# Two transformer layers on one core: GpSimd's power for the first reciprocal deviations, another order around the layers' seam, and small state products

## The chip, the cores and the metric

One core of one Trainium2 chip runs the whole program. The metric is the device time of one execution in microseconds (us). It is given as the median of several executions. TensorE is called PE here, VectorE DVE, ScalarE ACT, GpSimd POOL and SyncE SP, as in the profile.

## The reference

16 sequences of 256 tokens, 128 channels, go through two layers in float32. Each layer adds to its input an attention part and a part of eight experts, both of the normalised input:

```python
xn = _layernorm(x)                               # (x - mean) / sqrt(var + 1e-5)
x = x + attention_softmax_causal_16_heads(xn) + experts_top2_of_8(xn)
xn = _layernorm(x)
# layer 1, first part: retention with a decay, 8 heads of 16 channels
scores = einsum('bnhd,bmhd->bhnm', q, k) * decay[h, n - m]   # causal
ret = einsum('bhnm,bmhd->bnhd', scores, v)       # normalised per head, then gated and projected
out = (silu(xn @ W1) + ret * gn_w + gn_b) @ W2
# layer 1, second part: all 8 experts on all tokens, weighed by gates
probs = softmax(xn @ Wr + br)                    # gate = probs where the sorted running sum < 0.8
y = relu(xn @ W1[e] + b1[e]) @ W2[e] + b2[e]     # 128 -> 512 -> 128, for each e
x = x + out + sum_e gate[e] * y[e]
```

## The kernel before

All work is written out by hand. Each of the five engines has its own program, and counters (semaphores) tie them together: `pe.wait_ge(f_lo, n - 2)` holds PE and all that stands behind it on PE. An engine's order is therefore the order of its code.

**Layer 0** runs in 64 groups of four heads (`G0 = 64`), four groups to a sequence, in numbered slots. Each engine's `slot(g)` does its part of group g or of its neighbours: PE the scores, DVE the row maxima (`row_max_late`, `row_max_early`), ACT the exponential of a group into `probs`, POOL the causal cut of it (`cut_off`), PE the product with the values (`weigh`). Slots 0 to 9 also choose the two best experts of every token on DVE and POOL (`mark_best`, `pick_first`, `choose`, `count`; `COUNT` and `MARK` say in which slots). The experts of layer 0 come between groups 38 and 39 (`middle`). Six more slots (`TAIL0`, 64 to 69) finish the last groups, and the first normalised sequences of layer 1 are already made there.

**Layer 1's normalisation** takes the variance of 24 token tiles at once (`EARLY`, sequences 0 to 11) and of the last 8 later (`LATE`). In the kernel before, `deviation1` takes the root of it on ACT, which loads ACT's table for the square root first. `shift_of` takes the reciprocal on DVE, and `normalise(b, u)` applies it on ACT.

**Layer 1** is a row of 256 units, `UNITS = NB * E * FC`: 8 blocks of 512 tokens, 8 experts, 4 chunks of 128 hidden channels. `hidden(n)` is three products of 512 columns (a float32 product as three products of high and low parts), ACT takes the relu (`hidden_unit`, `f_h`), DVE the rest that f_h leaves (`split_unit`, `f_l`), and `output(n)` is three products more. `hidden(n)` waits for `f_lo >= n - 2`, so it is at most three units ahead of DVE. Sixteen units are a window, in which one sequence's retention is woven in between the units (`between`, by the table `when`): `scores1`, `products_qk`, `products_p`, `weigh1`, `sum_state` and so on. `sum_state` makes the product of keys and values of a sequence's first half, a 128x128 product of which `own_head` keeps the eight 16x16 blocks on the diagonal, and `weigh1` multiplies the queries by it.

**The expert weights of layer 1** come one expert after another over SP's queue, in code order: `load_raw(e, 0)`, then `w1_first` for e (one buffer; it waits for `centred`, the subtraction on POOL that uses it up), then `load_raw(e, 1)`. POOL's `centre(e)` subtracts `w1_first`, ACT's `high_w1(e)` rounds, POOL's `low_w1(e)` takes the rest. The gates of a block are worked out by a chain over POOL, DVE and ACT (`add_bias`, `less_max`, `exponentials`, `gate_sum`, `weigh_probs`, `compare`, `order_probs`, `keep_experts`), go out to memory (`keep_gates`), and come back spread over all partitions, 256 KB for each expert (`load_gate`). The first `LATER` experts of block 0 are multiplied by their gates afterwards on POOL (`gate_later`).

## Time and profile before

| | |
|---|---|
| median of 3 executions | 781.25 us (780.51 to 782.44) |
| the profiled execution's own time | 780.9 us |
| span of its trace | 779.1 us |
| busy PE, DVE, ACT, POOL | 718.4, 557.7, 441.0, 349.7 us |
| granted clock of PE, mean | 0.976 of full speed |

The span runs from the first to the last instruction of the trace; the execution's own time has 1.8 us around it. The matmuls' ends are modelled, so a PE that is shown busy is not always at its peak.

### The profile page before, as it was taken

To read this page: it belongs to the slowest core of one execution; us is meant where nothing else is said; L and a number is where in the kernel's file an instruction comes from. 1 tells how busy PE (TensorE), PEld (TensorE's weight loads), DVE (VectorE), ACT (ScalarE), POOL (GpSimd) and SP (SyncE) were. 2 spreads that over 40 slices of the span, in tenths; PEclk is the share of its full clock that TensorE was granted. 3 is DMA by queue.
4 is the path that set the end of the run, shared out by engine and by line. 5 is a ranking of instruction groups with operands and counts; after the bars stand their busy time and mean duration, and the time that the engine had idled before them with its cause. 6 is when DMAs were issued, how large, how long until landed. Compare 5 with 4: busy or idle time off the path is not lost.

```text
span 779.1 us, 16902 instructions
## 1 busy us (share of the span) xinstructions
PE 718.4 (92%) x5932; PEld 528.3 (68%) x5932; DVE 557.7 (72%) x1151; ACT 441.0 (57%) x821; POOL 349.7 (45%) x497
## 2 busy tenths in 40 slices
PE   5788788998899977779999999999999999999997
PEld 4644445556755536657877877877877878877775
DVE  6877997885688845549767767767767767776674
ACT  5745665775576665366555565565555555554442
POOL 3765644783758875176224224225224224223222
PEclk9998999999999988979999999999999999999999
DMA  6974655431144442531200210310410410400310
GB/s 189 266 222 133 177 143 201 149 106 41 59 123 124 122 131 64 127 122 41 70 30 12 83 39 5 82 42 1 82 42 1 92 33 2 95 28 12 85 42 14
DMA packets 64243, 66.85 MB, mean 86 GB/s; under 512 B 6689, under 2 KB 42273, under 8 KB 64161
## 3 DMA queue, kind: packets, MB, share of 16 engines
q1 hardware_dynamic: 62560, 63.40, 28.8%
q0 software_dynamic: 1024, 2.12, 1.0%
q8 instruction: 49, 0.80, 0.4%
q10 hardware_dynamic: 576, 0.27, 0.1%
q14 instruction: 34, 0.27, 0.1%
HBM read 47.62 MB, written 17.99 MB: 84 GB/s over the span
## 4 chain that ended last, share of the span: by engine, by line
PE 70%; DVE 8%; POOL 7%; DMA 5%; issue 3%; ACT 3%; SPq 2%; POOLq 0%; ACTq 0%; DVEq 0%
PE ps L1890 24%; PE ps L2096 22%; DVE m L1350 3%; PE ps L2007 2%; PE ps L1809 2%; PE ps L1713 2%; DMA qk_parts<-qk_p 2%; DMA w_first<-in_w_first 2%; POOL probs L696 2%; POOL x L679 2%; PE ps L1958 2%; PE ps L1923 1%; PE ps L1723 1%; PE ps L1719 1%; PE ps L2023 1%
## 5 line engine op out<-in xcount | busy, mean ns | idle before, releaser
L1571 DVE SCALAR_TENSOR_TENSOR f_l<-ps,f_h 128x512 fp32r<-128x512 f32 x256 | 176.0, 688 | 133.7 <-ACT f_h L1064 133.1
L1064 ACT ACTIVATE f_h<-ps 128x512 fp32r<-128x512 f32 x256 | 152.6, 598 | 182.1 <-PE ps L1890 178.1
L1890 PE MATMUL ps<-x_hl,w_h 128*128 128x512 f32 x512 | 194.6, 401 | 11.7 <-DVE f_l L1571 10.1
L829 POOL TENSOR_TENSOR acc<-acc,yt 128x512 f32<-128x512 f32 x56 | 72.7, 1298 | 196.9 <-DVE yt L1588 196.8
L1890 PEld LDWEIGHTS ps<-x_hl,w_h 128*128 128x128 f32 x512 | 98.0, 191 | 36.9 <-DVE f_l L1571 11.3
L969 ACT ACTIVATE probs<-ps 128x1536 f32<-128x1536 f32 x64 | 92.9, 1451 | 39.3 <-PE ps L1732 38.7
L2096 PE MATMUL ps<-f_h,w_h 128*128 128x512 f32 x256 | 108.1, 422 | 0.0
L696 POOL TENSOR_SCALAR_AFFINE_SELECT probs<-probs 128x512 f32<-128x512 f32 x128 | 78.7, 640 | 64.9 <-ACT probs L969 64.7
L1890 PE MATMUL ps<-x_hl,w_l 128*128 128x512 f32 x256 | 102.4, 400 | 0.0
L2096 PE MATMUL ps<-f_h,w_l 128*128 128x512 f32 x256 | 102.1, 399 | 0.0
L2096 PE MATMUL ps<-f_l,w_h 128*128 128x512 f32 x256 | 101.3, 396 | 0.0
L1350 DVE TENSOR_REDUCE m<-ps 128x4 f32<-128x1024 f32 x64 | 78.0, 1219 | 9.7 <-PE ps L1723 9.6
L2096 PEld LDWEIGHTS ps<-f_h,w_h 128*128 128x128 f32 x256 | 48.5, 190 | 12.8 <-issue 3.2
L1890 PEld LDWEIGHTS ps<-x_hl,w_l 128*128 128x128 f32 x256 | 49.2, 192 | 11.0
L2096 PEld LDWEIGHTS ps<-f_l,w_h 128*128 128x128 f32 x256 | 48.5, 189 | 11.8
L2096 PEld LDWEIGHTS ps<-f_h,w_l 128*128 128x128 f32 x256 | 48.7, 190 | 7.5
L1588 DVE SCALAR_TENSOR_TENSOR yt<-ps,b,gate_b 128x512 f32<-128x512 f32 x54 | 40.5, 750 | 6.3 <-PE ps L2096 3.1
L1343 DVE TENSOR_REDUCE m<-ps 128x4 f32<-128x512 f32 x64 | 43.5, 680 | 0.4 <-PE ps L1719 0.4
L1508 DVE TENSOR_TENSOR sc<-ps,upto 128x512 f32<-128x512 f32 x64 | 43.6, 681 | 0.0
L1809 PE MATMUL ps<-probs,v_ring 128*16 128x256 f32 x512 | 41.4, 395 | 0.7 <-ACT wvn L951 0.5
L1732 PE MATMUL ps<-q_st,k_st 49*128 49x128 bf16 x256 | 36.2, 222 | 2.9 <-DMA q_st<-m_neg 2.9
L1713 PE MATMUL ps<-mask_qk,ident_h 128*128 128x256 bf16 x128 | 25.5, 281 | 14.6 <-DVE m L1350 12.2
(234 smaller groups left out, 1349.8 us busy)
## 6 DMA issues: line engine op xcount, KB each, us to landing
gate_b<-gate_rows SPq DMA_DIRECT2D x64, 256.0 KB, 3.6
qk_parts<-qk_p SPq DMA_DIRECT2D x16, 512.0 KB, 3.8
k_st<-qk_parts SPq DMA_DIRECT2D x64, 96.0 KB
q_st<-qk_parts SPq DMA_DIRECT2D x64, 96.0 KB
y_tok<-zero SPq DMA_DIRECT2D x8, 512.0 KB, 3.0
w_raw<-in_w_e SPq DMA_DIRECT2D x16, 256.0 KB, 3.2
x_rows<-xn_rows SPq DMA_DIRECT2D x8, 260.0 KB, 3.4
w_up<-in_w_up SPq DMA_DIRECT2D x8, 256.0 KB, 2.7
```

The source lines that it names most:

```text
L696: nc.gpsimd.affine_select(tiles, tiles, pattern=[[0, GH], [1, P]], compare_op=ALU.is_ge, fill=0.0, base=0, channel_multiplier=-1)\
L829: nc.gpsimd.tensor_tensor(acc[:, j % 2, :], acc[:, j % 2, :], yt[:, i % 3, :], ALU.add).then_inc(summed, 1)
L969: nc.scalar.activation(probs[:, at(g, HELD), :, :], ps[:, 3:6, :], ACT.Exp, scale=float(D) ** -0.5)\
L1064: nc.scalar.activation(r32(f_h[:, n % 4, :]), ps[:, n % 3, :], ACT.Relu).then_inc(f_hi, 1)
L1343: nc.vector.tensor_reduce(m8[:, at(g, 2), :, 0], ps[:, first, :].rearrange("p (h k) -> p h k", h=GH), AX.X, ALU.max).then_inc(early_max, 1)
L1350: nc.vector.tensor_reduce(m8[:, at(g, 2), :, 1], ps[:, first + 1:first + 3, :].rearrange("p c (h k) -> p (c h) k", h=2), AX.X, ALU.max).th ...
L1508: nc.vector.tensor_tensor(sc[:, h, :, :], ps[:, 4 + h, :].rearrange("p (k t) -> p k t", t=P), upto[:, :].unsqueeze(1).broadcast_to([P, 4, ...
L1571: nc.vector.scalar_tensor_tensor(out=r32(f_l[:, n % 4, :]), in0=ps[:, n % 3, :], scalar=0.0, in1=f_h[:, n % 4, :], op0=ALU.max, op1=ALU.su ...
L1713: nc.tensor.matmul(scores_at(g)(c).rearrange("p (h k) -> p h k", h=2)[:, :, P:S], ident_h[:, :], mask_qk[:, :].unsqueeze(1).broadcast_to([ ...
L1809: nc.tensor.matmul(ps_o[32 * h:32 * h + 2 * HD0, :], v_ring[:, u, 0, k * GH + h, :], probs[:, at(g, HELD), 1 + h // 2, h % 2 * S:(h % 2 + ...
L1890: last = nc.tensor.matmul(dst, r32(lhs[i]), r32(rhs[j]), start=(k == 0), stop=(k == 2))
L2096: last = nc.tensor.matmul(ps[:, 3, :], r32(w[i]), r32(fs[:, n % 4, :]), start=(c == 0 and k == 0), stop=(c == FC - 1 and k == 2))
```

## The change

Layer 0's choice of experts is spread over one slot more (`COUNT` 5, `MARK` 10, `mark_best` and `pick_first` in slots 0 to 3). The reciprocal deviations of `EARLY` are one instruction on POOL, `var` to the power of -0.5; the variance of `LATE` moves to DVE's unit 29 and its root to ACT's unit 34, behind a root that ACT takes there anyway. The first sequences of layer 1 are normalised, turned and multiplied among the last slots. The two products with the state become four products of 32 channels each. On SP, `keep_gates(0)` and the first gate loads move behind the loads of experts 5 and 6, and on POOL the later gating moves from unit 13 to units 17 to 20. Some banks of PSUM are given out anew. Cut to its core:

```diff
-COUNT = 4
-MARK = 9
+COUNT = 5
+MARK = 10
-LATER = 3
+LATER = 4
...
-        def ps_t1(b): return ps[:, b if b < 2 else 0 if b == 2 else 4, 0:S]
+        def ps_t1(b): return ps[:, b if b < 2 else 3 if b == 2 else 4, 0:S]
-        def bank_p1(b): return 4 if b in (0, 2) else 6
-        def ps_state(b): return ps[:, 4 if b == 0 else 7, 0:P]
+        def bank_p1(b): return 4 if b in (0, 2) else 0 if b == 1 else 6
+        def ps_state(b): return ps[:, 6 if b == 0 else 7, 0:2 * HD1]
...
-            usual = {"values_by_scores": 9, "turn_z": 8, "put_z": 11, "put_o": 12, "turn_o": 12, "project": 13, "heads": 15,
+            usual = {"values_by_scores": 8, "turn_z": 8, "put_z": 11, "put_o": 12, "turn_o": 12, "project": 12, "heads": 15,
...
-                if e == 3:
+                if e == 5:
                     keep_gates(0)
+                if e == 6:
                     for k in range(4):
                         load_gate(0, k)
-                if e >= 5:
-                    load_gate(0, e - 1)
-            load_gate(0, E - 1)
+            for k in range(4, E):
+                load_gate(0, k)
...
+                if num(g) == G0 - 4:
+                    nc.gpsimd.memset(minus_half[:, :], -0.5).then_inc(padded, 1)
+                if num(g) == G0 - 1:
+                    pool.wait_ge(padded, 1)
+                    pool.wait_ge(var_ready, 1)
+                    nc.gpsimd.tensor_tensor(rstd[:, EARLY], var[:, EARLY], minus_half[:, 0:1].broadcast_to([P, EARLY.stop]), ALU.pow).then_inc(rstd_ready, 1)
+                    add_experts(B - 1)
+                    centre(0)
...
             values(0)
+            low_w1(1)
+            put_ones(0)
             add_bias(0)
             less_max(0)
-            put_ones(0)
-            low_w1(1)
+            values(1)
             weigh_probs(0)
-            values(1)
             order_probs(0)
...
-                        if n == max(FC * e - 10, 0):
+                        if n == (0, 2, 6, 12, 16, 20)[e - 2]:
                             centre(e)
...
-                if n == 13:
-                    for g in range(LATER):
+                for g in range(LATER):
+                    if n == (17, 17, 19, 20)[g]:
                         gate_later(g)
                         add_expert(g)
...
+                if num(g) == G0 - 1:
+                    act.wait_ge(rstd_ready, B + 2)
+                    normalise(0, 0)
                 if within(g, G0):
                     act.wait_ge(st_done, num(g) + 1)
...
                 if num(g) == G0:
-                    deviation1(1, EARLY)
+                    high_x(0)
+                    normalise(1, 1)
...
-            deviation1(2, LATE)
             put_gate(0)
+            halve(0)
             high_w1(1)
-            halve(0)
+            put_gate(1)
             high_x(2)
-            put_gate(1)
...
                     root_of(b)
+                    if b == 1:
+                        deviation1(2, LATE)
...
+                if n == G0 - 1:
+                    shift_of(1, EARLY)
+                if n == LAST - 1:
+                    dve.wait_ge(late_in, (LATE_IN + 5) * 16)
+                    put_qk(0)
+                    put_values(0)
+                    put_qk(1)
...
-                if n in (1, 2):
-                    pick_first(n - 1)
-                if n in (0, 1):
-                    mark_best(n)
+                if n in (1, 3):
+                    pick_first(n // 2)
+                if n in (0, 2):
+                    mark_best(n // 2)
...
-                if n == G0 - 2:
+                if n == G0 - 3:
                     variance_of(EARLY)
...
+                if n == 29:
+                    for b in range(B - 2, B):
+                        stats_of(b)
+                    variance_of(LATE)
+                if n == 38:
+                    shift_of(2, LATE)
...
-                nc.tensor.matmul(ps_state(b), k_tok[:, b % 2, :], v1[:, b % 4, 0, 0:D], start=True, stop=True).then_inc(state_mm, 1)
+                for h in range(GH):
+                    pair = slice(32 * h, 32 * h + 32)
+                    last = nc.tensor.matmul(ps_state(b)[pair, :], k_tok[:, b % 2, pair], v1[:, b % 4, 0, pair], start=True, stop=True)
+                last.then_inc(state_mm, 1)
...
-                nc.tensor.matmul(ps_o1[:, P:S], states[:, b % 3, :], qk1[:, b % 3, 0, P:S], start=False, stop=False, skip_group_check=True)
+                for h in range(GH):
+                    pair = slice(32 * h, 32 * h + 32)
+                    nc.tensor.matmul(ps_o1[pair, P:S], states[pair, b % 3, :], qk1[pair, b % 3, 0, P:S], start=False, stop=False, skip_group_check=True)
...
-            products_qk(0)
-            products_p(0)
             products_qk(1)
+            products_p(1)
             transposes(2)
+            hidden(0)
+            hidden(1)
             pe.wait_ge(x_attn, B)
-            products_p(1)
             sum_state(0)
-            pe.wait_ge(state_put, 1)
+            pe.wait_ge(v1_put, 1)
             products_p(2)
             sum_state(1)
-            hidden(0)
-            hidden(1)
```

`shift_of(1, ...)` no longer takes the reciprocal itself, and `memset` of `v1_ring` stays where it was. `normalise(1, 1)` and `high_x` are each a slot or two earlier in the tail.

**PE, the first hidden units.** In the kernel before, PE's rows from the last products of sequence 2 on (`w1_p` with `x_hl` is `products_p`, `w1_h` and `w1_l` with `x_hl` are hidden units, `k_tok` is `sum_state`):

```order
L1984 MATMUL ps<-v1,k_tok 128x128 [waits v1_put,k_put]
L1890 MATMUL ps<-x_hl,w1_h 128x512 [waits xl_put,ones_put,w1_lo]
L1890 MATMUL ps<-x_hl,w1_l 128x512
L1890 MATMUL ps<-x_hl,w1_h 128x512 x2
L1890 MATMUL ps<-x_hl,w1_l 128x512
L1890 MATMUL ps<-x_hl,w1_h 128x512
L1890 MATMUL ps<-x_hl,w1_h 128x512 [waits qk1_put]
L1890 MATMUL ps<-x_hl,w1_l 128x512
L1890 MATMUL ps<-x_hl,w1_h 128x512
L1890 MATMUL ps<-x_hl,w1_h 128x512 [waits f_lo]
L1890 MATMUL ps<-x_hl,w1_l 128x512
L1890 MATMUL ps<-x_hl,w1_h 128x512
```

In the changed kernel, the rows in the same place behind `hidden(1)`:

```order
L1995 MATMUL ps<-v1,k_tok 32x32 x3
L1899 MATMUL ps<-w1_p_hi,x_hl 128x392 [waits xl_put,v1_put]
L1899 MATMUL ps<-w1_p_hi,x_hl 128x392
L1899 MATMUL ps<-w1_p_lo,x_hl 128x392
L1899 MATMUL ps<-w1_p_hi,x_hl 128x264 x2
L1899 MATMUL ps<-w1_p_lo,x_hl 128x264
L1995 MATMUL ps<-v1,k_tok 32x32 [waits v1_put,k_put]
L1995 MATMUL ps<-v1,k_tok 32x32 x3
L1899 MATMUL ps<-x_hl,w1_h 128x512 [waits qk1_put]
L1899 MATMUL ps<-x_hl,w1_l 128x512
L1899 MATMUL ps<-x_hl,w1_h 128x512
L1899 MATMUL ps<-x_hl,w1_h 128x512 [waits f_lo]
```

The products of sequence 2 stood ahead of `hidden(0)` and `hidden(1)` and now stand between `hidden(1)` and `hidden(2)`; the last row is `hidden(3)`, the first that waits for `f_lo`.

**POOL, the last groups of layer 0.** Before (`probs` rows are the cuts of a group, `y_top` and `xn_rows` the addition of the experts to a sequence, `w1_first` a `centre`, `w1_l` a `low_w1`):

```order
L696 AFFINE_SELECT probs<-probs 128x4x128 [waits exp_done]
L696 AFFINE_SELECT probs<-probs 128x512
L696 AFFINE_SELECT probs<-probs 128x4x128 [waits exp_done]
L696 AFFINE_SELECT probs<-probs 128x512
L679 TENSOR_TENSOR x<-x,y_top 128x256 [waits x1_half,gathered1]
L679 TENSOR_TENSOR x<-x,xn_rows 128x256 [waits x1_half]
L831 MEMSET v1_ring 128x1024
L748 TENSOR_TENSOR w_raw<-w_raw,w1_first 128x512 [waits first_in,raw_in0,padded]
L753 TENSOR_TENSOR w1_l<-w_raw,w1_h 128x512 [waits w1_hi]
L748 TENSOR_TENSOR w_raw<-w_raw,w1_first 128x512 [waits first_in,raw_in2]
```

And now:

```order
L697 AFFINE_SELECT probs<-probs 128x4x128 [waits exp_done]
L697 AFFINE_SELECT probs<-probs 128x512
L716 TENSOR_TENSOR rstd<-var,minus_half 128x24 [waits var_ready,padded]
L680 TENSOR_TENSOR x<-x,y_top 128x256 [waits x1_half,gathered1]
L680 TENSOR_TENSOR x<-x,xn_rows 128x256 [waits x1_half]
L754 TENSOR_TENSOR w_raw<-w_raw,w1_first 128x512 [waits first_in,raw_in0]
L697 AFFINE_SELECT probs<-probs 128x4x128 [waits exp_done]
L697 AFFINE_SELECT probs<-probs 128x512
L838 MEMSET v1_ring 128x1024
L759 TENSOR_TENSOR w1_l<-w_raw,w1_h 128x512 [waits w1_hi,padded]
```

The power, the addition and the first `centre` stand ahead of the last group's two cuts.

**SP, the weights and gates of block 0.** Before, from expert 3's loads on (`w1_first` and the two `w_raw` rows around it are one expert):

```order
L511 DMA w1_first<-in_w1_first 128x512 [waits centred]
L504 DMA w_raw<-in_w2_e 128x512 [waits w2_lo]
L569 DMA gate_rows<-gT 4x8x128 [waits gt_put]
L564 DMA gate_b<-gate_rows 128x512 [waits gates_out]
L564 DMA gate_b<-gate_rows 128x512 x3
L504 DMA w_raw<-in_w1_e 128x512 [waits w1_lo]
L511 DMA w1_first<-in_w1_first 128x512 [waits centred]
L504 DMA w_raw<-in_w2_e 128x512 [waits w2_lo]
L504 DMA w_raw<-in_w1_e 128x512 [waits w1_lo]
L511 DMA w1_first<-in_w1_first 128x512 [waits centred]
L504 DMA w_raw<-in_w2_e 128x512 [waits w2_lo]
L564 DMA gate_b<-gate_rows 128x512 [waits raw_gated,yv]
```

And now, from expert 5's loads on:

```order
L505 DMA w_raw<-in_w1_e 128x512 [waits w1_lo]
L512 DMA w1_first<-in_w1_first 128x512 [waits centred]
L505 DMA w_raw<-in_w2_e 128x512 [waits w2_lo]
L570 DMA gate_rows<-gT 4x8x128 [waits gt_put]
L505 DMA w_raw<-in_w1_e 128x512 [waits w1_lo]
L512 DMA w1_first<-in_w1_first 128x512 [waits centred]
L505 DMA w_raw<-in_w2_e 128x512 [waits w2_lo]
L565 DMA gate_b<-gate_rows 128x512 [waits gates_out]
L565 DMA gate_b<-gate_rows 128x512 x3
L505 DMA w_raw<-in_w1_e 128x512 [waits w1_lo]
L512 DMA w1_first<-in_w1_first 128x512 [waits centred]
L505 DMA w_raw<-in_w2_e 128x512 [waits w2_lo]
```

The gates' way out and the four loads that wait for it stood between experts 3 and 4; they now stand behind expert 5 and behind expert 6.

## Rows read from the trace of the kernel before

**Rows 1.** Windows: busy us of each engine, PEclk is the granted clock.

```profile
core 0 of [0], span 779.1 us
...
330.00:335.00 5.00, 1.11 (x3) 0.92 (x4) 0.69 (x1) 3.37 (x6) 3.07 (x3) 0.50 0.43 141
379.59:408.36 28.77, 28.77 (x194) 23.14 (x194) 19.77 (x38) 16.75 (x31) 6.51 (x11) 1.00 0.19 50
```

**Rows 2.** Timeline of PE, 302 to 350: start, us, work [idle before].

```profile
302.67 0.77 PE L1890 MATMUL ps<-x_hl,w_h 128*128 128x512 f32 x1 [1.62 <-issue]
...
311.70 0.50 PE L1890 MATMUL ps<-x_hl,w_h 128*128 128x512 f32 x1
...
333.88 0.79 PE L1890 MATMUL ps<-x_hl,w_h 128*128 128x512 f32 x1 [7.04 <-DVE f_l L1571]
...
348.58 0.50 PE L1890 MATMUL ps<-x_hl,w_h 128*128 128x512 f32 x1 [3.08 <-DVE f_l L1571]
...
349.47 1.09 PE L2007 MATMUL ps<-qk 16*128 16x128 f32 x16
```

**Rows 3.** Timeline of SP, issues of 318 to 322; then the landing times of w_first.

```profile
318.73 1.96 SPq L564 DMA_DIRECT2D gate_b<-gate_rows  x4
...
321.21 1.10 SPq L511 DMA_DIRECT2D w_first<-in_w_first  x1
...
DMA to landing us min/median/max: 2.7/2.9/9.0
```

**Rows 4.** Timeline of POOL, 284 to 331.

```profile
284.26 1.23 POOL L696 TENSOR_SCALAR_AFFINE_SELECT probs<-probs 128x512 f32<-128x512 f32 x2 [2.98 <-ACT probs L969]
...
301.60 0.98 POOL L761 MEMSET x_hl<- 1x512 f32 x2
302.55 1.27 POOL L753 TENSOR_TENSOR w_l<-w_raw,w_h 128x512 fp32r<-128x512 f32 x1
...
330.30 1.26 POOL L748 TENSOR_TENSOR w_raw<-w_raw,w_first 128x512 f32<-128x512 f32 x1 [14.30 <-DMA w_first<-in_w_first]
```

**Rows 5.** Timeline of ACT, 285 to 347.

```profile
285.86 1.28 ACT L1015 ACT_TABLE_LOAD   x1
...
300.87 0.38 ACT L1049 ACTIVATE sg<-ps 128x256 f32<-128x256 f32 x1 [0.64 <-PE ps L1890]
301.27 1.28 ACT L1098 ACT_TABLE_LOAD   x1
...
346.54 0.23 ACT L1098 ACTIVATE g_x<-g_l 128x32 f32<-128x32 f32 x1 [4.44 <-POOL g_l L791]
```

**Rows 6.** Timeline of DVE, 304 to 312.

```profile
304.05 0.48 DVE L1551 TENSOR_TENSOR g_gt<-g_p 128x256 f32<-128x256 f32 x1 [0.82 <-POOL g_p L796]
...
310.95 0.69 DVE L1571 SCALAR_TENSOR_TENSOR f_l<-ps,f_h 128x512 fp32r<-128x512 f32 x1 [3.00 <-ACT f_h L1064]
```

**Rows 7.** Timelines of DVE and PE, 58 to 61.

```profile
58.26 0.42 DVE L1236 TENSOR_REDUCE r_s<-r_b 128x32 f32<-128x256 f32 x1
...
60.33 0.61 PE L1713 MATMUL ps<-mask_qk,ident_h 128*128 128x256 bf16 x2 [2.56 <-DVE m L1350]
```

**Rows 8.** Chain of waits in one steady window, 395 to 402: start, us, work.

```profile
395.50 0.57 PE ps L2018 x16
396.07 0.42 PE ps L2020 x2
...
397.06 0.91 PE ps L2096 x3
397.97 0.70 PE ps L1890 x3
...
401.69 0.22 PE ps L1984 x2
```

**Rows 9.** Groups of POOL by line and shape, whole run.

```profile
L748 POOL TENSOR_TENSOR w_raw<-w_raw,w_first 128x512 f32<-128x512 f32 x8 | 10.7, 1332 | 16.2 <-DMA w_first<-in_w_first 16.0
...
L785 POOL TENSOR_TENSOR g_l<-v,rb 128x32 f32<-128x32 f32 x8 | 2.0, 254 | 18.7 <-DVE v L1494 18.7
```

82 lines of the change are left out of this document (36 added, 46 removed).

## The prediction

> **What bounds the kernel now.** I read the slices of the page first, then windows, then PE's timeline where they dip. From about 350 us to the end PE has no idle time: a window of sixteen units takes 28.8 us and PE is busy in all of it, at the full clock [rows 1]. Nothing but PE's own work can move that part. Between 282 and 352 us, where layer 0 ends and the weights of layer 1 come in, PE waits again and again, and this is where the change works. Three places count [rows 2]. The first hidden unit starts at 302.67 us, after 1.6 us of idle, at half clock: its first product shows 0.77 us where the same product at 311.70 shows 0.50. At 333.88 PE has been idle for 7.0 us. At 348.58 it has been idle for 3.1 us. The window that starts with `scores1(1)` begins only at 349.47.
>
> The 7.0 us: PE and DVE stand because ACT stands in `high_w1(4)`, which waits for POOL's `centre(4)`, and POOL has been idle for 14.3 us until `w1_first` landed [rows 4]. SP issued that load at 321.21, right behind the four gate loads of 318.73 (1 MB) [rows 3]. It took 9.0 us to land where the median is 2.9 [rows 3]. After it PE works at the lower of its two clocks: 0.50 granted from 330 to 335 [rows 1]. The 3.1 us: ACT waited 4.4 us for POOL's `less_max(1)` before the exponential of the gates, with the relus queued behind it [rows 5]. POOL was late because `centre(4)` was late and because unit 13's gating stands ahead of `less_max(1)` in its code.
>
> **The seam up to the first hidden unit.** Removed from ACT: the load of the square root's table, 1.28 us at 285.86 [rows 5], and its root; from DVE a reciprocal. In their place POOL takes the power of 128x24 numbers. No row shows this operation. From below: an addition of 128x32 takes 0.25 us [rows 9]. From above I take POOL's longest arithmetic row, 1.3 us for 128x512 [rows 9]; a power is more work on each number than a subtraction, so I take the upper value, 1.3 us. It begins when POOL has done the cuts of group 62, at 281.3 us (2.98 us before the row at 284.26) [rows 4]; the variance, moved one slot earlier, is ready before that. Its result is at 282.6, the shift 0.3 us later, and ACT's two normalisations (0.9 us) end at 283.8. Only then does ACT take group 63's exponential, about 1.1 us later than before, and POOL adds 1.5 + 1.3 us (addition, `centre(0)`) ahead of its cuts, which start near 285.5 instead of 284.26. All behind it slips by about 1.2 us, but products, turns and normalisations of sequences 0 and 1 now run in gaps of the tail. I followed each engine's new order with durations of the old rows. `put_gate(0)` ends at 296.8, `low_w1(1)` at 299.2, and `put_ones(0)` (0.98 us [rows 4]), for which `hidden(0)` waits, at 300.2 instead of 302.6. **Term 1: -2.5 us.** PE is idle for some 1.9 us just before, as it was before, so I take the lower clock for the first units again.
>
> **From hidden(0) to hidden(5).** This stretch gets longer. In the kernel before, a chain runs through it: `put_gate(2)` at 300.87 and ACT's table load at 301.27 [rows 5], exponential, sum on DVE, `weigh_probs`, `compare` at 304.05 [rows 6], `order_probs`, `centre(2)`, `high_w1(2)`, relu, the rest of unit 2 at 310.95 to 311.64 [rows 6], then `hidden(5)` at 311.70 [rows 2]. From table load to `hidden(5)` that is 10.4 us, and the load began 1.4 us ahead of `hidden(0)`. Now `products_p(2)`, which `put_gate(2)` needs, stands behind `hidden(0)` and `hidden(1)`. At the low clock these take 2.6 us (two times 0.70 us for three products [rows 8], nearly doubled), `sum_state(0)` 0.4, the 1968 columns of `products_p(2)` 1.7, and `put_gate(2)` 0.4: the table load starts 5.1 us behind `hidden(0)`. The chain is 0.7 us shorter, since `low_w1(1)` (1.27 us at 302.55) no longer stands ahead of `weigh_probs` [rows 4, 6]. So `hidden(5)` follows `hidden(0)` by 5.1 + 9.7 = 14.8 us instead of 9.0. **Term 2: +5.8 us** (3.8 at the full clock). A new wait of PE, of about 3 us, should show before `hidden(3)`, which waits for `f_lo`; `compare(0)` stands ahead of `split_unit(0)` on DVE.
>
> **From hidden(5) to scores1(1).** Before: 311.70 to 349.47, 37.8 us [rows 2]. A steady window gives 28.8 us from one `scores1` to the next [rows 1], 3.3 of them before the unit that answers to `hidden(5)`; the first window also lacks a turn, a projection and a sum, 1.0 us. That makes 24.5 us if nothing waits. Does anything? `w1_first` now meets only the expert loads: `centre(2)`, a load of 2.9 us, `centre(3)`, a load, `centre(4)` ends some 6.5 us behind `hidden(5)`, and ACT comes to `high_w1(4)` 7 us behind it. Each further expert has 7 us of PE's time for a cycle of 4.2. `less_max(1)` stands ahead of the gating now. **Term 3: -13.3 us.** It includes both idle times and the half-speed stretches behind them.
>
> **Window 1.** Before, it began at the low clock and took 1.3 us more than a steady one. The gating is here now: seven instructions of 1.3 us on POOL in units 17 to 20, beside `centre(7)`, the heads and `order_probs(1)`. I count `low_w1(7)` done about 1.2 us before PE needs it for `hidden(28)`. The late statistics give DVE some 1.8 us in unit 29; DVE is busy 19.8 us of a window's 28.8 [rows 1]. **Term 4: -1.3 us.**
>
> **The steady windows.** `weigh1` shows 0.57 us for sixteen instructions, 0.42 for the full-array product with the state and another long row behind [rows 8]. Eight more small instructions at the same 0.036 us would be 0.28: -0.14. `sum_state` costs 0.22 us [rows 8]; as eight small ones 0.28, and 0.2 for changing to small tiles and back, as the 0.91 us against 0.70 show behind `weigh1` [rows 8]: +0.26. The projection now stands with other small products and saves one change, -0.1. The sum is 0.0 a window, give or take 0.12, so ±2 us over 16 windows. **Term 5: 0.**
>
> **Slots 0 to 4.** DVE's `mark_best(1)`, two instructions of 0.42 us, moves from ahead of a row maximum that PE was idle 2.6 us for to behind it [rows 7]. **Term 6: -0.8 us.** Should the clock then not fall, 2 us more come back.
>
> Sum: -2.5 + 5.8 - 13.3 - 1.3 + 0 - 0.8 = -12.1, and 780.9 of the profiled execution becomes 768.8. The median stands 0.35 us above that execution: 769 us, own range 764.5 to 773 (clock at full in term 2, -2; a fall avoided in term 6, -2; windows ±2; the power down to 0.25 us, -1, or up to 3 us, +1.7).
>
> **Rivals.**
> - *The small state products don't overlap.* The four products with the state use rows and columns of one block each and write one bank. Nothing in the trace runs like this: `scores1` uses a bank for each block of rows. If they go one by one, eight at 0.11 us (`sum_state`'s 0.22 for two [rows 8]) are 0.88 instead of 0.42, +0.46 in each of 16 windows: 776.4. Chance 0.12. The Trainium skill speaks for it: TensorEngine Tiling (Array Packing), Gotcha 1: PSUM Pressure, says that different row tiles cannot access the same bank at once. No row here shows it.
> - *The power costs some 6 to 12 us.* Every microsecond over 1.3 delays ACT's last exponential by as much: 774 to 780. Chance 0.1. The Trainium skill (GPSIMD Engine Reference, 2.1 Instruction dispatch) has about 6 us for the first call of a freshly loaded kernel; POOL's first kinds here show no such gap.
> - *The power is slower still, and the change loses.* Place: ACT's wait for `rstd_ready` ahead of group 63's exponential. From 1.3 + 12.1 = 13.4 us on it decides; at 20 us the time is 787.5. For it: the work is some 3,000 powers, and POOL is the only engine of which no root or power is seen. Against it: all its two-operand rows follow their size alone. Chance 0.05.
> - *POOL's backlog moves instead of going.* If the gate loads land 3 us late or the order of units 17 to 22 is tighter than I count, `low_w1(7)` holds PE at `hidden(28)` for 3 to 5 us: 772 to 774. Chance 0.1.
> - *The gate loads were not the cause.* Then `centre(4)` waits as long behind `w1_first` and only terms 1, 2 and 4 act: 780 to 783. Against it: 9.0 us beside a median of 2.9. Chance 0.03.
>
> Forecast 0.6. A difference under 0.3% can't be told from none here. Faster by more: 0.92; within 0.3%: 0.03; slower: 0.05. The range goes from 764.5 to 776.5 us, so that the first rival is in it.
>
> **What would show it.** In the changed profile: the power near 1.3 us at about 281; `hidden(0)` near 300; a wait of 3 us before `hidden(3)`; no wait for `w1_first` over 3 us; `scores1(1)` near 339.5; windows of 28.8 us. The forecast is wrong if the power is long, if a window is 29.2 us or more, or if PE is idle between 315 and 375.

## The result, and the profile of the changed kernel

| | before | changed |
|---|---|---|
| median of 4 executions each, one chip | 781.17 us (780.51 to 782.44) | 775.4 us (774.58 to 777.66) |
| profiled execution, its span | 780.9, 779.1 us | 777.66, 775.9 us |
| busy PE, DVE, ACT, POOL | 718.4, 557.7, 441.0, 349.7 us | 719.5, 558.4, 438.4, 355.2 us |

The medians differ by 5.8 us, where 12.2 were forecast (the ratio is 0.9929, with a 95% interval of 0.9904 to 0.9953). The time is inside the range of 764.5 to 776.5 us, and the sign is right; the size is a little under half.

Five marks on PE split the difference of the two traces, which is only 3.2 us (779.1 to 775.9): the profiled execution of the changed kernel was the slowest of its four. Against the forecast of -12.1 that leaves 8.9 us to explain. The first column of numbers is the kernel before [rows 1, 2], the second the changed one.

| stretch on PE | before | changed | measured | forecast |
|---|---|---|---|---|
| start to scores of group 63 | 281.87 | 277.44 | -4.4 | -0.8 (term 6) |
| from there to `hidden(0)` | 20.8 | 24.9 | +4.1 | -2.5 (term 1) |
| `hidden(0)` to `hidden(5)` | 9.0 | 13.8 | +4.8 | +5.8 (term 2) |
| `hidden(5)` to `scores1(1)` | 37.8 | 24.6 | -13.2 | -13.3 (term 3) |
| window 1 | 30.05 | 34.60 | +4.55 | -1.3 (term 4) |
| `scores1(2)` to the end | 399.6 | 400.6 | +1.0 | 0 (term 5) |

The first mark flatters the change: PE waited 2.94 us for a load ahead of group 63's scores in the kernel before and 1.57 us in the changed one. At the scores of group 62 (277.17 and 274.10 us) the changed kernel is 3.1 us ahead, and from there to `hidden(0)` it takes 28.2 us instead of 25.5, +2.7. Group 63's scores in the kernel before:

```profile
281.87 0.26 PE L1732 MATMUL ps<-q_st,k_st 49*128 49x128 bf16 x1 [2.94 <-DMA q_st<-m_neg]
```

PE's timeline in the changed kernel; start, us, work, and in brackets the idle time before it and what ended it:

```profile
277.44 0.26 PE L1737 MATMUL ps<-q_st,k_st 49*128 49x128 bf16 x1 [1.57 <-DMA q_st<-m_neg]
...
285.77 0.66 PE L1939 MATMUL ps<-ident,wv_tok 128*128 128x128 f32 x2 [6.10 <-ACT o_ring L945]
...
302.30 0.47 PE L1899 MATMUL ps<-x_hl,w_h 128*128 128x512 f32 x1 [1.67 <-POOL x_hl L767]
...
309.38 0.79 PE L1899 MATMUL ps<-x_hl,w_h 128*128 128x512 f32 x1 [3.07 <-DVE f_l L1573]
...
316.10 0.39 PE L1899 MATMUL ps<-x_hl,w_h 128*128 128x512 f32 x1
...
340.67 0.73 PE L2019 MATMUL ps<-qk 16*128 16x128 f32 x16
...
347.38 0.50 PE L2112 MATMUL ps<-f_l,w_h 128*128 128x512 f32 x1 [1.38 <-DVE f_l L1573]
...
350.03 0.79 PE L1899 MATMUL ps<-x_hl,w_h 128*128 128x512 f32 x1 [1.45 <-DVE f_l L1573]
```

The idle times of 7.04 and 3.08 us [rows 2] are gone. In their place stand 6.10 us ahead of 285.77, 3.07 us ahead of `hidden(3)` (309.38, as forecast), and two of 1.4 us in window 1, where none was forecast.

POOL shows the cause of the first, and a part of the last two:

```profile
278.18 4.20 POOL L716 TENSOR_TENSOR rstd<-var,minus_half 128x24 f32<-128x24 f32 x1
...
339.15 1.30 POOL L823 TENSOR_TENSOR acc<-acc,gate_b 128x512 f32<-128x512 f32 x1 [2.66 <-DMA gate_b<-gate_rows]
340.93 1.27 POOL L823 TENSOR_TENSOR yt<-yt,gate_b 128x512 f32<-128x512 f32 x1 [0.48 <-DMA gate_b<-gate_rows]
...
343.53 0.24 POOL L802 TENSOR_TENSOR g_p<-g_x,g_s 128x32 f32<-128x32 f32 x1
...
347.82 1.27 POOL L754 TENSOR_TENSOR w_raw<-w_raw,w_first 128x512 f32<-128x512 f32 x1
```

The power takes 4.20 us, not 1.3. At 339.15 POOL has waited 2.66 us for the gates of the first expert; `weigh_probs(1)` (343.53) and `centre(7)` (347.82) stand behind. On ACT and on DVE:

```profile
283.15 0.88 ACT L1028 ACTIVATE xn_ring<-x,shift,rstd 128x128 f32<-128x128 f32 x2 [6.66 <-DVE shift L1428]
283.94 1.43 ACT L978 ACTIVATE probs<-ps 128x1536 f32<-128x1536 f32 x1
285.26 0.37 ACT L945 ACTIVATE o_ring<-ps 128x256 f32<-128x256 f32 x1
...
349.13 0.63 ACT L1039 ACTIVATE w_h<-w_raw 128x512 fp32r<-128x512 f32 x1 [3.66 <-POOL w_raw L754]
```

```profile
343.81 1.50 DVE L1553 TENSOR_TENSOR g_gt<-g_p 128x256 f32<-128x256 f32 x1 [1.89 <-POOL g_p L802]
345.23 1.50 DVE L1554 TENSOR_TENSOR g_ge<-g_p 128x256 f32<-128x256 f32 x1
346.65 0.68 DVE L1573 SCALAR_TENSOR_TENSOR f_l<-ps,f_h 128x512 fp32r<-128x512 f32 x1
```

ACT stands 6.66 us for the shift, with the exponential of group 63 and the copy of `o_ring` behind it, for which PE waits until 285.77. In window 1, DVE waits for `weigh_probs(1)`, then makes two comparisons of 1.50 us, and only then the rest `f_l` that PE waits for at 347.38; ACT waits 3.66 us for `centre(7)` with the relus behind it, and PE waits a second time. SP tells why the gates were late (the last two lines are SP's next load of `w1_first`, expert 7's, and the time that it took to land):

```profile
334.85 0.33 SPq L505 DMA_DIRECT2D w_raw<-in_w_e  x1
335.22 1.86 SPq L565 DMA_DIRECT2D gate_b<-gate_rows  x4
...
337.61 1.22 SPq L512 DMA_DIRECT2D w_first<-in_w_first  x1
...
DMA to landing us min/median/max: 9.9/9.9/9.9
```

The four gate loads stand behind expert 6's second raw load, which waits for DVE's `low_w2(4)`. Behind the four stands the `w1_first` of expert 7. It was 9.9 us on its way and landed at about 347.5, where the median of the eight is 3.1: what held `centre(4)` in the kernel before [rows 3] now happens to `centre(7)`, which started at 347.82. POOL's rows show no wait for it, because POOL was busy with the late gating until that moment. So `centre(7)` had two causes to be late that end within 0.3 us of each other, the gating ahead of it on POOL and its own load.

Windows (columns as in [rows 1]) show the clock:

```profile
345.00:350.00 5.00, 2.21 (x9) 1.15 (x7) 4.96 (x8) 1.34 (x3) 4.92 (x5) 0.91 0.71 196
350.00:355.00 5.00, 4.97 (x16) 4.19 (x17) 5.00 (x9) 1.88 (x5) 4.76 (x6) 0.50 0.20 52
...
375.27:404.14 28.87, 28.87 (x203) 23.06 (x203) 20.05 (x39) 16.85 (x32) 6.47 (x11) 1.00 0.18 49
```

After the two waits the granted clock is 0.50, the lower level, for five microseconds: window 1 loses 5.7 us against a steady one, 2.8 of them idle; the rest goes with the lower clock. The steady window is 0.10 us longer than before.

### The profile page after: what moved, and what is told of

Same layout as the page of the kernel before. It is cut to its first block, busy times and chain, and to the rows that moved or that the text cites. A ratio compares the mean times of both kernels' runs of the same rounds, so it can differ in the third digit from the quotient of the medians.

```text
span 775.9 us, 17290 instructions
## 1 busy us (share of the span) xinstructions
PE 719.5 (93%) x6124; PEld 528.2 (68%) x6124; DVE 558.4 (72%) x1150; ACT 438.4 (57%) x819; POOL 355.2 (46%) x500
## 4 chain that ended last, share of the span: by engine, by line
PE 74%; DVE 9%; POOL 7%; issue 3%; ACT 3%; DMA 3%; SPq 1%; POOLq 0%; DVEq 0%; ACTq 0%
PE ps L1899 26%; PE ps L2112 23%; DVE m L1354 3%; PE ps L2019 2%; POOL x L680 2%; POOL probs L697 2%; PE ps L1718 2%; PE ps L1814 2%; PE ps L1967 2%; DMA qk_parts<-qk_p 1%; PE ps L1932 1%; PE ps L1728 1%; PE ps L2030 1%; PE ps L2037 1%; PE ps L1724 1%
## 5 line engine op out<-in xcount | busy, mean ns | idle before, releaser
L1814 PE MATMUL ps<-probs,v_ring 128*16 128x256 f32 x512 | 41.4, 395 | 1.6 <-issue 1.1
L1718 PE MATMUL ps<-mask_qk,ident_h 128*128 128x256 bf16 x128 | 25.3, 280 | 13.2 <-DVE m L1354 11.2
```

What stands on the lines that cost most here:

```text
L1718: nc.tensor.matmul(scores_at(g)(c).rearrange("p (h k) -> p h k", h=2)[:, :, P:S], ident_h[:, :], mask_qk[:, :].unsqueeze(1).broadcast_to([ ...
L1814: nc.tensor.matmul(ps_o[32 * h:32 * h + 2 * HD0, :], v_ring[:, u, 0, k * GH + h, :], probs[:, at(g, HELD), 1 + h // 2, h % 2 * S:(h % 2 + ...
```

## The experiments

Kernels of one group below ran on the same chip, each with the kernel before beside it. The chips differ by up to 1.8% in absolute times (the kernel before had medians of 794.2, 780.7 and 794.9 us), so ratios to the kernel before and stretches inside a trace are compared.

**Group 1, price: what a power costs.**

```diff
+            TRIED = ((24, ALU.pow), (6, ALU.pow), (1, ALU.pow), (12, ALU.pow), (96, ALU.pow), (24, ALU.mult))
+                for k, (count, op) in enumerate(TRIED):
+                    if n == 100 + 10 * k:
...
+                            nc.gpsimd.tensor_tensor(tried[:, k, 0:count], var[:, 0:count], minus_half[:, 0:1].broadcast_to([P, count]), op)
```

> The changed kernel with six more instructions on POOL in the steady windows of layer 1, where POOL is idle most of the time, each into a buffer that nobody reads: the power of 128x24, 128x6, 128x1, 128x12 and 128x96 numbers and a product of 128x24. The profile of the changed kernel has one power, 128x24 in 4.20 us. If a power costs by its elements, the five show about 4.2, 1.1, 0.2 to 0.3, 2.1 and 16.8 us. If it costs a fixed time whatever the shape, all five show about 4.2. If the 4.20 us were the price of a first call (code or a table that has to come in), the first one here, which is the second of the program, is far below 4.2, near 0.25 us. The product should show about 0.25 in each case.

Groups of POOL by shape (count, busy us, mean ns):

```profile
L898 POOL TENSOR_TENSOR tried<-var,minus_half 128x96 f32<-128x96 f32 x1 | 15.6, 15636 | 0.0
L896 POOL TENSOR_TENSOR tried<-var,minus_half 128x24 f32<-128x24 f32 x2 | 4.4, 2198 | 0.0
L717 POOL TENSOR_TENSOR rstd<-var,minus_half 128x24 f32<-128x24 f32 x1 | 4.2, 4204 | 0.0
L896 POOL TENSOR_TENSOR tried<-var,minus_half 128x12 f32<-128x12 f32 x1 | 2.3, 2270 | 0.0
L896 POOL TENSOR_TENSOR tried<-var,minus_half 128x6 f32<-128x6 f32 x1 | 1.3, 1337 | 0.0
L896 POOL TENSOR_TENSOR tried<-var,minus_half 128x1 f32<-128x1 f32 x1 | 0.6, 550 | 0.0
```

The two of 128x24 at L896 are a power (4.17 us, the longest) and the product (0.22 us, the shortest). So the cost is 0.16 us for each column and 0.4 us besides, and the second call is as long as the first. A power costs by its elements; it is not the price of a first call. The whole kernel took 801.5 us in its one execution: 16 us of power in window 8 hold up everything (that window took 37.9 us, where a steady one takes 28.9), so such an instruction is not free even where POOL is idle three quarters of the time.

**Group 1, power_first: only six columns ahead of the last group.**

```diff
+        FIRST, SECOND = slice(0, 6), slice(6, EARLY.stop)
-                    nc.gpsimd.tensor_tensor(rstd[:, EARLY], var[:, EARLY], minus_half[:, 0:1].broadcast_to([P, EARLY.stop]), ALU.pow).then_inc(rstd_ready, 1)
+                    power_of(FIRST)
...
+            pool.wait_ge(rstd_ready, B + 2)
+            power_of(SECOND)
             pool.wait_ge(padded, 2)
             low_w1(0)
```

> The changed kernel, where the power ahead of the last group's cuts takes only the six columns that sequences 0 to 2 need, and the other eighteen are done behind the clearing of v1_ring, where POOL was idle for 6.35 us. Cost by elements: the first power takes 1.1 us instead of 4.20, the shift comes at 279.3 instead of 282.4, PE's idle time of 6.10 us shrinks to about 3, hidden(0) starts near 299.2 instead of 302.3, and the end comes 3 us earlier than in the changed kernel (772.4 us if that one is 775.4). Fixed cost: the first power takes 4.2 us again, nothing moves, the same time within 0.5 us. A third reading, that hidden(0) waits for something else at the seam (the weights' rounding, values), would show the power short and hidden(0) still at 301.5 or later: a gain under 1 us.

Measured: 787.34 us, ratio 0.9929 (0.9901 to 0.9956). The powers took 1.37 and 3.22 us, PE's idle time fell to 4.40 us:

```profile
290.18 0.21 PE L1745 MATMUL ps<-q_st,k_st 49*128 49x128 bf16 x1 [1.29 <-DMA q_st<-m_neg]
295.97 0.66 PE L1947 MATMUL ps<-ident,wv_tok 128*128 128x128 f32 x2 [4.40 <-ACT o_ring L952]
...
312.38 0.47 PE L1907 MATMUL ps<-x_hl,w_h 128*128 128x512 f32 x1 [1.68 <-POOL x_hl L772]
```

From the scores of group 63 to `hidden(0)` it is 22.2 us, 2.7 less than the 24.9 of the changed kernel's trace: the forecast of "cost by elements". One pair of traces is weak for that, since the seven traces with the full power spread from 22.8 to 25.0; the table under term 1 below takes the clock apart from it. In the whole time no gain is shown: the ratio is that of the changed kernel (0.9929; 0.994 in `after_again`), where 3 us less would have been 0.989.

**Group 1, gates_ahead: the gate loads before expert 6's second raw load.**

```diff
                 sp.dma_start(w1_first[:, :], a["w1_first"][:, ds(e, 1), :].rearrange("p o f -> p (o f)")).then_inc(first_in, 16)
+                if e == 6:
+                    for k in range(4):
+                        load_gate(0, k)
                 load_raw(e, 1)
...
-                if e == 6:
-                    for k in range(4):
-                        load_gate(0, k)
```

> The changed kernel, where SP issues the four gate loads between expert 6's w1_first and its second raw load, for which SP stands still until 334.85 us. My theory: window 1 lost 5.7 us because POOL waited until 339.15 and 340.93 for gate_b and was then late with weigh_probs(1) (DVE stood 1.89 us) and with centre(7) (ACT stood 3.66 us). With the loads issued at about 330.5 and landed by 335, the first later gating starts near 336.6, centre(7) about 2.8 us earlier, ACT's wait falls under 1 us, PE's two idle times of 1.38 and 1.45 us go or nearly go and the clock does not fall: window 1 takes 29 to 31 us instead of 34.6, and the end comes 4 to 5 us earlier. Rival, the order of POOL's units is too tight whenever the gates come: window 1 stays over 33 us and the gain is under 1.5 us. Rival, the loads now delay w1_first of expert 6 (9.0 us to land in the kernel before): window 0 gets longer than 30.5 us and the sum gains nothing.

Measured: 785.56 us, ratio 0.9895 (0.9872 to 0.9918). POOL and ACT in window 1 (it starts at 352.84 here, 12.2 us later on the clock than in the changed kernel's trace):

```profile
347.37 1.29 POOL L754 TENSOR_TENSOR w_raw<-w_raw,w_first 128x512 f32<-128x512 f32 x1
348.61 1.30 POOL L823 TENSOR_TENSOR acc<-acc,gate_b 128x512 f32<-128x512 f32 x1
349.99 1.30 POOL L823 TENSOR_TENSOR yt<-yt,gate_b 128x512 f32<-128x512 f32 x1
...
357.38 1.30 POOL L754 TENSOR_TENSOR w_raw<-w_raw,w_first 128x512 f32<-128x512 f32 x1
```

```profile
358.72 0.63 ACT L1039 ACTIVATE w_h<-w_raw 128x512 fp32r<-128x512 f32 x1 [1.08 <-POOL w_raw L754]
```

No wait for `gate_b` is left; `centre(7)` follows `centre(6)` by 10.0 us instead of 12.6, ACT's wait falls from 3.66 to 1.08 us, PE idles once in window 1, 0.53 us, and the window takes 29.60 us instead of 34.60. Window 0 stays at 29.66: `w1_first` is not delayed. The order of the units was not too tight. The edit also brings the `w1_first` of expert 7 away from the gate loads: no `w1_first` takes more than 4.8 us to land here. So the run shows that the place of the gate loads costs these us, and does not tell POOL's late gating from the late `w1_first`. The other traces agree: six with the late loads (the changed kernel's two, `price`, `power_first`, `old_choice`, `full_state`) have a window 1 of 33.0 to 34.8 us, six with the early ones (`gates_ahead`, `both`, `exp_first`, `best2`, `best3`, `root_act`) 29.6 or 29.7. In the whole time the ratio is 0.0034 to 0.0045 under the changed kernel's, 2.7 to 3.6 us, less than the 4 to 5 expected.

**Group 1, old_seam: the seam's order as before, in the changed kernel.**

```diff
-                if e == 5:
+                if e == 3:
                     keep_gates(0)
-                if e == 6:
                     for k in range(4):
                         load_gate(0, k)
...
-                        if n == (0, 2, 6, 12, 16, 20)[e - 2]:
+                        if n == max(FC * e - 10, 0):
...
-                    if n == (17, 17, 19, 20)[g]:
+                if n == 13:
+                    for g in range(LATER):
```

> The changed kernel with the order of the seam's weights and gates as before: keep_gates(0) and the first gate loads behind expert 3, the others after experts 5 to 7, centre(e) in the old units, three experts gated later in unit 13. My theory, that this part alone brought the gain of terms 3 and 4: window 0 takes 39 to 42 us again instead of 29.7, with PE idle about 7 us for w1_first, window 1 about 30 us instead of 34.6; the end comes 4 to 7 us later than in the changed kernel, near 780. If instead the loads are not the cause (the tail's order or the choice of slots brought the gain), window 0 stays near 30 us and the time within 1 us of the changed kernel's.

Measured: 800.43 us, ratio 1.0089 (1.0061 to 1.0117), slower than the kernel before. Window 0 took 44.11 us, window 1 30.57: together 74.7, against 64.6 in the kernel `power_first` on the same chip. This order alone is worth 10.1 us net of the late gates. PE idles 7.59 us in window 0 again; POOL waited 14.71 us for a `w1_first` that was issued at 336.18, right behind the four gate loads of 333.69, and landed only at about 345.6. With the old order the rest of the change is a loss of 6 to 7 us, in part because that order costs more here than in the kernel before (window 0 of 44.1 us against 41.4).

**Group 2, both: the two mends together** (the edits of `power_first` and `gates_ahead`).

> The changed kernel with two edits already tried alone: the short first power (hidden(0) 2.7 us closer to the last group's scores) and the gate loads ahead of expert 6's second raw load (window 1 29.6 us instead of 34.6). If the two losses are independent, they add: hidden(0) about 22.2 us behind scores(63) instead of 24.9, window 1 29.6 us, and the end 7.7 us earlier than the changed kernel, a ratio of 0.983 to 0.984 to the kernel before. Rival, that the earlier first unit only makes the expert weights late (they come over one queue): window 0 then grows by 1 to 3 us and the ratio is 0.986 to 0.989.

Measured: 768.53 us, ratio 0.9858 (0.9835 to 0.9882), worse than the 0.983 to 0.984 expected, though on the same chip it is 7.9 us under `full_state` (below), which has neither mend. Group 63's scores to `hidden(0)` 19.9 us, window 0 29.74, window 1 29.56. Both gains stand side by side, and the weights did not become late. The first stretch is 2.3 us shorter than the 22.2 us of `power_first`: 0.9 us of it because the power starts 0.1 us behind group 63's scores and not 1.0, and 1.4 us with the clock: PE's granted clock was back at 0.89 in the second five microseconds behind the idle time, in the other trace 0.50:

```profile
280.00:285.00 5.00, 2.54 (x21) 1.32 (x21) 0.43 (x2) 2.56 (x6) 4.68 (x6) 0.50 0.34 108
285.00:290.00 5.00, 3.68 (x37) 2.71 (x34) 1.61 (x7) 2.96 (x8) 2.73 (x2) 0.89 0.01 2
```

```profile
298.00:303.00 5.00, 3.88 (x35) 2.15 (x28) 0.76 (x3) 1.42 (x4) 2.94 (x1) 0.50 0.03 11
```

**Group 2, exp_first: group 63's exponential ahead of the normalisation** (on top of `both`; POOL's cuts of group 63 move ahead of `add_experts` and `centre(0)` too).

```diff
-                if num(g) == G0 - 1:
-                    act.wait_ge(rstd_ready, B + 2)
-                    normalise(0, 0)
                 if within(g, G0):
                     act.wait_ge(st_done, num(g) + 1)
...
+                if num(g) == G0 - 1:
+                    act.wait_ge(rstd_ready, B + 2)
+                    normalise(0, 0)
```

> The kernel of the last expectation with one more edit: in slot 63 ACT takes the exponential of group 63 ahead of normalise(0, 0), and POOL its cuts ahead of the addition and centre(0), directly behind the short power. In the changed kernel ACT stood 6.66 us there for the shift, with the exponential and the next copies of o_ring behind it. My theory: the copy behind the exponential is what PE waited 6.1 us for (4.4 with the short power); it now comes 3 us earlier, PE idles about 1.5 us there and hidden(0) comes 1.5 to 3 us earlier in relation to scores(63), about 20 us behind it. Rival, the path to hidden(0) goes over the normalised tokens, not over the exponential: PE's idle time moves to the turns of sequence 0 and 1, and hidden(0) comes less than 0.7 us earlier.

Measured: 769.18 us, ratio 0.9855 (0.9833 to 0.9877). PE's idle time for `o_ring` fell to 1.89 us, but `hidden(0)` comes 19.8 us behind group 63's scores, as in `both` (19.9), and the time is the same. My theory fell, the rival holds: the exponential was what PE was seen to wait for, and the chain that sets `hidden(0)` does not go over it. A gain of 0.7 us may hide behind the clock: from the end of the power to `hidden(0)` it is 19.1 us here, against 19.8 in `power_first`, both at the lower clock.

**Group 2, best2: the order around the first units** (on top of `exp_first`).

```diff
+            put_ones(0)
             low_w1(1)
-            put_ones(0)
...
+                if n == 0:
+                    put_gate(2)
+                    exponentials(0)
...
                 split_unit(n)
+                if n == 0:
+                    gate_sum(0)
+                    put_state(1)
+                    compare(0)
```

> The kernel of the last expectation with the order around the first units changed: on POOL put_ones(0), for which hidden(0) waited 1.67 us, ahead of low_w1(1); on ACT put_gate(2) and the exponential of the gates behind the first relu; on DVE gate_sum, put_state(1) and compare behind the first split_unit. My theory of term 2: PE's 3.07 us before hidden(3) are a wait for split_unit(0), which stood behind compare(0) and the gates' chain; it goes (under 0.7 us is left), hidden(0) comes 1.2 us earlier, and scores1(0) comes 3 to 4 us earlier; a ratio of 0.974 to 0.978 if the rest follows. Rival, the weights of experts 2 to 4 hold PE then: the waits of 1.00 and 0.81 us in window 0 grow to 2 to 4 us, window 0 takes 31 to 33 us and less than 1.5 us of the gain is left at scores1(1).

Measured: 769.62 us, ratio 0.9849 (0.983 to 0.9869). PE, then ACT:

```profile
297.26 0.47 PE L1910 MATMUL ps<-x_hl,w_h 128*128 128x512 f32 x1 [0.47 <-POOL x_hl L773]
...
301.93 0.51 PE L1910 MATMUL ps<-x_hl,w_h 128*128 128x512 f32 x1 [0.65 <-DVE f_l L1582]
...
310.41 0.80 PE L1910 MATMUL ps<-x_hl,w_h 128*128 128x512 f32 x1 [4.12 <-DVE f_l L1582]
```

```profile
308.52 0.63 ACT L1047 ACTIVATE w_h<-w_raw 128x512 fp32r<-128x512 f32 x1 [5.36 <-POOL w_raw L760]
```

The ratio is that of `both`, where 0.974 to 0.978 was expected: nothing is gained. The 3.07 us ahead of `hidden(3)` fell to 0.65, as my theory had it, and window 0 grew to 34.58 us, more than the rival had it. The place is another than the rival's: not a load, but ACT's `high_w1(2)`, which stood 5.36 us for `centre(2)`, and that stood on POOL behind the four instructions of `order_probs(0)`. Term 2's wait had covered this one.

**Group 2, full_state: the products with the state at full width, in the changed kernel.**

```diff
-                for h in range(GH):
-                    pair = slice(32 * h, 32 * h + 32)
-                    last = nc.tensor.matmul(ps_state(b)[pair, :], k_tok[:, b % 2, pair], v1[:, b % 4, 0, pair], start=True, stop=True)
-                last.then_inc(state_mm, 1)
+                nc.tensor.matmul(ps_state(b), k_tok[:, b % 2, :], v1[:, b % 4, 0, 0:D], start=True, stop=True).then_inc(state_mm, 1)
```

(and `weigh1`'s product in the same way)

> The changed kernel with the two products with the state as before: one 128x128 product for sum_state and one for weigh1 in place of four of 32 channels each, with the mask and the state at their old sizes; the order of PE's work stays as changed. Windows of the changed kernel take 28.87 and 28.55 us, of the kernel before 28.77 and 28.45. If the small products are the 0.10 us, windows fall to 28.77 and 28.45 here and the time by 1.1 to 1.6 us. If they save and another part of the new order costs, windows rise to 28.95 to 29.2 and the time by 1 to 4 us. If they cost nothing either way, the windows stay at 28.87 and 28.55, and the 0.10 belongs to the moved steps (turn_sum shows 0.59 us where it showed 0.35 to 0.44).

Measured: 776.4 us, ratio 0.994 (0.992 to 0.9959); windows 28.79 and 28.45 us, so the small products are the 0.10 us. From `scores1(2)` to the end it is 399.8 us instead of 400.6; the ratio is too coarse to show this. The chain of waits in a steady window (start, us, work), the changed kernel first:

```profile
397.38 0.20 PE ps L1995 x8
397.57 0.59 PE ps L2075 x4
398.16 0.45 PE ps L2065 x4
...
419.31 0.35 PE ps L2034 x8
```

```profile
398.80 0.22 PE ps L1993 x2
399.02 0.44 PE ps L2070 x4
399.46 0.45 PE ps L2060 x4
...
420.58 0.42 PE ps L2029 x2
```

Eight small instructions of `sum_state` show 0.20 us, the full ones 0.22; in `weigh1` 0.35 and 0.42. What is lost stands behind: `turn_sum`, the first full product after the small ones, shows 0.59 instead of 0.44.

**Group 3, after_again: the changed kernel as the measure.**

> The changed kernel itself once more, as the measure for the other three on the same chip. Expected: a ratio of 0.993 to the kernel before; scores(63) to hidden(0) about 24.9 us, window 0 29.7 us, window 1 34.6 us.

Measured: 789.68 us, ratio 0.994 (0.9918 to 0.9962). Scores of group 63 to `hidden(0)` 23.8 us, windows 29.87 and 32.98: the first and the last are 1.1 and 1.6 us shorter than in the first trace of the same kernel. PE's granted clock was back earlier (0.86 against 0.50 in the five microseconds from 13 us ahead of `hidden(0)`; 0.80 against 0.50 behind the waits of window 1). A difference of 1.5 us between two traces in these stretches need therefore be no effect of an edit.

**Group 3, old_choice: the choice of experts in the old slots.**

```diff
-COUNT = 5
-MARK = 10
+COUNT = 4
+MARK = 9
...
-                if n in (0, 2):
-                    mark_best(n // 2)
+                if n in (0, 1):
+                    mark_best(n)
```

> The changed kernel with the choice of experts in the old slots (COUNT 4, MARK 9, mark_best in slots 0 and 1, pick_first in 1 and 2). Term 6 was forecast at 0.8 us, 2.8 if the clock does not fall; layer 0 of the changed kernel showed 3 us at the middle and 4.4 us at scores(63) against the kernel before. My theory now: the spread is worth the whole 3 us at the middle, since PE idles 2.6 us again at about 60 us and the clock falls again between 60 and 100 us; this kernel is then 2.5 to 3.5 us slower than the changed one. Rival: the clock there falls or stays by chance or by another difference of layer 0, and the spread is worth the 0.8 us of the shorter wait: 0.5 to 1.2 us slower, with the granted clock of 60 to 100 us at 1.00 here as well.

Measured: 793.49 us, ratio 0.9991 (0.9973 to 1.0008), 3.8 us over `after_again`. The windows of this kernel, of `after_again` and of `best2`, which has the new slots:

```profile
60.00:100.00 40.00, 33.27 (x423) 17.23 (x424) 33.94 (x62) 24.25 (x40) 22.41 (x35) 0.92 0.53 158
```

```profile
60.00:100.00 40.00, 35.19 (x469) 19.07 (x468) 35.04 (x67) 26.28 (x44) 24.90 (x37) 0.96 0.58 170
```

```profile
60.00:100.00 40.00, 35.38 (x460) 18.61 (x458) 34.34 (x66) 25.14 (x43) 24.04 (x36) 0.92 0.58 163
```

PE idled 2.57 us at 60 us instead of 1.78, the mean clock was 0.92 instead of 0.96, and PE ran 423 instructions in 40 us instead of 469. The step is 3 to 4 us, as the theory had it. Its cause is not mainly the clock, though: `best2` has the low clock of the old slots (0.92) and still runs 460 instructions. The distance on PE from the first scores of group 0 to those of group 21 parts the two:

| slots | granted clock, 60 to 70 us | traces | group 0 to group 21 |
|---|---|---|---|
| old | 0.67, 0.68 | `old_choice`, kernel before | 75.6, 75.5 us |
| new | 0.68, 0.69 | `best2`, `old_seam` | 73.4 us |
| new | 0.83 | eight others and `after_again` | 72.3 to 72.5 us |
| new | 1.00 | the changed kernel's first trace | 72.1 us |

At the same clock the new slots give 2.0 us, and the smaller fall of the clock 1.1 us more.

**Group 3, best3: all mends, and centre(2) ahead of weigh_probs(0).**

```diff
-                        if n == (0, 2, 6, 12, 16, 20)[e - 2]:
+                        if n == (-1, 2, 6, 12, 16, 20)[e - 2]:
...
             values(1)
+            centre(2)
             weigh_probs(0)
```

(with the edits of `power_first`, `gates_ahead`, `exp_first`, `best2` and `full_state`)

> The changed kernel with everything that the experiments point to: the short first power, group 63's exponential ahead of normalise(0, 0), put_ones(0) ahead of low_w1(1), put_gate(2) and the exponential of the gates behind the first relu, compare(0) behind the first split_unit, the gate loads ahead of expert 6's second raw load, the state products as one 128x128 product each, and new here centre(2) ahead of weigh_probs(0) on POOL. In the last kernel ACT stood 5.36 us for centre(2), which stood behind order_probs(0), and PE idled 4.12 us at 310.41. If that order was all that took the gain away, the wait falls under 1.5 us, window 0 takes 29.5 to 30.5 us, the steady windows take 28.78 and 28.45, and the ratio to the kernel before is 0.976 to 0.980. Rival, the expert weights' loads over SP's queue are the next bound: window 0 takes 31 us or more and the ratio is 0.981 to 0.984.

Measured: 778.81 us, ratio 0.9796 (0.9768 to 0.9824), 10.9 us under the changed kernel on the same chip. It is the fastest kernel of the study. Window 0 took 31.91 us, where 29.5 to 30.5 was expected and the rival had 31 or more: PE still idled 2.22 us at 322.59, behind ACT's 2.08 us for the next `centre`, `centre(3)`. It started at 320.62, right behind `order_probs(0)` and `low_w1(2)` on POOL, with no wait for a load, so the rival's cause is not this one. Whether `centre(3)` can be moved too was not tried.

**Group 3, root_act: ACT's root in place of the power** (the exponential of group 63 ahead of it, gates ahead).

```diff
-                    nc.gpsimd.tensor_tensor(rstd[:, EARLY], var[:, EARLY], minus_half[:, 0:1].broadcast_to([P, EARLY.stop]), ALU.pow).then_inc(rstd_ready, 1)
...
+                if num(g) == G0 - 1:
+                    deviation1(1, EARLY)
+                    act.wait_ge(rstd_ready, B + 2)
+                    normalise(0, 0)
...
-                if n == 2:
-                    dve.wait_ge(std_ready, B // 2 + 1)
-                    nc.vector.reciprocal(rstd[:, tiles], std[:, tiles]).then_inc(rstd_ready, 1)
+                dve.wait_ge(std_ready, B // 2 + n)
+                nc.vector.reciprocal(rstd[:, tiles], std[:, tiles]).then_inc(rstd_ready, 1)
```

> The changed kernel with the gate loads moved ahead as before and without GpSimd's power: ACT takes the root (with its table load of 1.28 us) in slot 63 behind the group's exponential, DVE the reciprocal, and normalise(0, 0) follows; the rest of the tail stays as changed. From rows: exponential 278.3 to 279.7, table 1.28, root 0.22, reciprocal and shift 0.5, so normalise(0, 0) starts near 282.0, where it started at 283.15 behind the full power and at 280.3 behind the short one. If that is so, scores(63) to hidden(0) takes 22 to 23.5 us, against 24.9 with the full power: the power of 24 columns on POOL is slower at the seam than the root that it replaced, by 1 to 2 us. Rival, the table has to be loaded once more for the gates or the exponential (1.28 us each): then 24 to 25 us, and the power is no loss. Window 1 29.6 us in both cases.

Measured: 783.16 us, ratio 0.986 (0.9827 to 0.9894). Scores of group 63 to `hidden(0)` 21.8 us. Seven traces with the full power (the changed kernel's two, `price`, `gates_ahead`, `old_seam`, `old_choice`, `full_state`) show 22.8 to 25.0, five with the short one 19.2 to 22.2. The one trace with the root is 1 us under the shortest of the full power, and some 3 us under the three with the same clock behind the idle time (24.9 to 25.0), of which the exponential's place may be 0.7 (`exp_first`). The ratio points the same way (0.986 against 0.9895 of `gates_ahead`, which has the full power and the same gate loads), but the intervals overlap and the exponential's place differs too: that the power of 24 columns is slower than the root it replaced is likely, not settled.

## Why the prediction was right in sign and wrong in size

Two steps failed above all, the price of the power in term 1 and the gates in term 4. Of the 8.9 us between forecast and trace, term 4 makes 5.9, terms 1 and 6 together 2.9, term 5 1.0, and term 2 takes 1.0 back.

**Term 1 failed, and in its size: "so I take the upper value, 1.3 us".** The power took 4.20 us. The longest arithmetic row of POOL was called the upper end, though it was a row of another operation; an operation that no row shows has no upper end in rows of cheaper ones. That a longer power makes `hidden(0)` later by as much is shown when the traces are taken from the end of the power on. The clock is PE's granted clock in the five microseconds from 13 us ahead of `hidden(0)`; `exp_first`, `best2`, `best3` and `root_act` are left out, since their edits change this stretch itself.

| trace | first power | its end to `hidden(0)` | clock |
|---|---|---|---|
| changed kernel, `gates_ahead`, `old_choice` | 4.20 us | 19.9 us | 0.50 to 0.53 |
| `power_first` | 1.37 us | 19.8 us | 0.55 |
| `after_again`, `price`, `old_seam` | 4.20 us | 18.4 us | 0.86, 0.87 |
| `both` | 1.37 us | 18.4 us | 0.82 |
| `full_state` | 4.20 us | 20.7 us | 0.50, and 2 us longer at the lower level |

At the same clock the rest of the stretch does not change with the length of the power, so the 2.9 us over 1.3 were lost in full. The term took the way to go over ACT's exponential and the copy of `o_ring`; they did stand behind it, but `exp_first` shows that `hidden(0)` hardly depends on them. The power itself started where the term had it, 4.1 us behind the scores of group 62. The term then had 17.6 us from its end to `hidden(0)`, and even at the better clock it is 18.4. Together: 2.9 us for the power and 2.3 us for what follows it, of which 1.5 goes with the clock and 0.8 has no cause shown. PE was idle 6.10 us at this place and worked at the lower clock until about 294 us; the term had only a slip of 1.2 us.

**Term 6 was mis-sized the other way.** Forecast -0.8, with 2 more "Should the clock then not fall"; undoing it costs 3.8 us in the whole time, and layer 0 came out 3.1 us ahead at group 62's scores (4.4 at group 63's, by the shorter wait for a load). The table under `old_choice` shows the step that failed: the 0.8 us counted only the wait at 60 us, and the new slots gave 2.0 us at an unchanged clock; the clock gave 1.1 to 1.4 more, not 2. Terms 1 and 6 together were forecast at -3.3 and gave -0.4, and `hidden(0)` stands at 302.30 where the sum of all had it 2.9 us earlier. The two errors hide each other in the time.

**Terms 2 and 3 held.** +4.8 for +5.8, with the wait of 3.07 us ahead of `hidden(3)` that was forecast as "about 3 us"; -13.2 for -13.3. The near hit of term 2 is in part luck: it took the lower clock for the first units, and PE had the full one there (`hidden(0)` shows 0.47 us for its first product, 0.77 before), for which the term gave +3.8. `scores1(1)` is at 340.67, 1.2 us behind the forecast. `old_seam` shows that the seam's order is the cause, with the 14.71 us wait for `w1_first` behind the gate loads back; it moves the loads, `centre` and the gating at once and does not part them. What the term did not say is that the wait of term 2 is cover: `best2` took it away and ACT's wait for `centre(2)` came out behind it.

**Term 4 failed: "I count `low_w1(7)` done about 1.2 us before PE needs it".** The count followed POOL's own instructions and never asked when the gates that they multiply by would land. The first lands at 339.15, since their issue stands behind a raw load that waits for DVE. Term 3's sentence "`w1_first` now meets only the expert loads" failed in window 1: expert 7's stands behind the four gate loads and landed only at about 347.5. The rival of a moved backlog, with a chance of 0.1, was this case, and its first condition ("if the gate loads land 3 us late") is what happened (2.66 us). Its place was wrong: not PE at `hidden(28)`, but DVE at `weigh_probs(1)` and ACT at `centre(7)`, some units earlier, where the relus are queued. Its price of 3 to 5 us was 5.0 (34.60 against 29.60 without the late loads; 3.4 by the trace of `after_again`).

**Term 5 was 1.0 us off, within its ±2.** The parts: `sum_state` -0.02 for a forecast of +0.06, `weigh1` -0.07 for -0.14, the change back to full products +0.15 for +0.2, and the change that moving the projection was to save, 0.1, did not come: it shows 0.45 us now and 0.44 before.

**The rivals.** "The small state products don't overlap" is refuted: in `weigh1` eight instructions show 0.35 us and not 0.88, 0.044 each where a full one takes 0.21. By the rule of the Trainium skill (TensorEngine Tiling (Array Packing), Gotcha 1: PSUM Pressure), that row tiles cannot access the same bank at once, the window would have been 0.46 us longer; the trace does not agree for these four diagonal tiles of 32x32. "The power costs some 6 to 12 us" did not happen at 4.20 us, but its rule, every microsecond over 1.3 as much later, held for `hidden(0)` at an equal clock (table above), though not by way of the exponential. The fixed first call of some 6 us that the Trainium skill gives (GPSIMD Engine Reference, 2.1 Instruction dispatch) is not seen: first call 4.20, second 4.17 us, and the first starts at 278.18 with no idle time ahead of it. Against "The gate loads were not the cause" stand `old_seam` and the 9.9 us of expert 7's `w1_first` behind the same loads. That the change loses was off: at 4.2 us the power was far from the 13.4 from which it would have decided.

## What to carry to other kernels

An operation that the trace does not show needs a price by elements, from a run of its own at two sizes, before its place is chosen; then give the critical place only the columns that are needed there. When work is moved to a later unit, follow its inputs as well as its engine: the queue on which they are issued, and what the issue stands behind; and ask which load stands behind it in turn. An idle time that is taken away uncovers the next one; read what the same engines do just behind it before counting the gain.

## What the runs showed of the hardware that was not expected

- A power on POOL costs 0.55, 1.34, 2.27, 3.22, 4.17 and 15.6 us for 1, 6, 12, 18, 24 and 96 columns of 128 partitions, where a product of 24 columns takes 0.22.
- DVE's comparisons of 128x256 took 1.50 us each at 343.81 and 345.23, while POOL's subtraction and product ran beside them, and 0.42 us each in `best2` at 302.94 and 303.28, where POOL was idle. The pairing holds in the rest of the changed kernel's trace: with POOL idle they took 0.41 to 0.43 us, and 0.45 or 0.46 where a POOL addition covered their first 0.2 us. Term 4's account of DVE (19.8 of 28.8 us) did not have this. No run here takes POOL's work away at that place, so this is a pairing, not a proof.
- An idle time of 1.77 to 1.79 us at about 60 us in layer 0 was followed by a granted clock of 1.00 from 60 to 100 us in the changed kernel's first trace, of 0.96 in nine others, `after_again` among them, and of 0.92 in `best2` and `old_seam`; 2.57 us were followed by 0.92 in `old_choice`. The length of this idle time alone does not tell how long the clock stays low, and the same order of work can differ by a microsecond or two from one execution to the next.
